# Hidden products of a mixture of experts: all three parts of each product in the same 160 PSUM columns, and the GELU reads PSUM

## The chip, the core and the metric

The kernel runs on one core of a Trainium2 chip. The metric is the device time of one launch in microseconds, the median of several runs. A core has TensorE (PE, with a weight load of its own that the profile lists as PEld), VectorE (DVE), ScalarE (ACT), GpSimd (POOL), SyncE (SP), and DMA queues.

## What is computed

The reference takes 1,250 nodes with 512 features, applies a layer norm, two graph convolutions and a three layer decoder, and adds the result to the input. The part that matters here comes after it: a dropless mixture of 8 experts over the first 512 tokens, two experts a token.

```
for e in range(NUM_EXPERTS):
    h = jax.nn.gelu(xg @ w1[e], approximate=False)
    y = jnp.where((bin_ids == e)[:, None], h @ w2[e], y)
w = expert_weights.reshape(-1)[order][:, None]
out = jnp.zeros((T, hs), x.dtype).at[token_ids].add(w * y)
```

Here `xg` are the normalised tokens sorted by expert, `w1` is 512 by 256 and `w2` 256 by 512 for each expert.

## The kernel before

The kernel is written by hand, engine by engine: each engine has a program of its own, in a fixed order, and the programs meet at semaphores. The graph part ends some 115 us into the span; the expert part, which the change touches, runs from there to the end.

**Tokens of an expert.** Each expert has 160 slots: 128 main slots, and 32 more (`MORE`) that hold what doesn't fit. Four experts (`TEAM`) share one tile of 128 for these extra slots, so there are two teams. The tokens of a slot list are gathered from memory by an indirect DMA (`gather`, L661), transposed by TensorE (`transpose_gathered`, L1859, and `transpose_tails`, L1869), and split in two parts: ScalarE copies the high part (`keep_gathered`, L1406 and L1411), and VectorE subtracts it from the transposed tokens to get the low part (`gathered_rest`, L1112 and L1116). The two parts of a tile lie side by side in `xg_t`, 160 columns each.

**Product up.** `up_slots(e)` makes the hidden units, 256 of them in two halves (m = 0, 1) of 128. Each half adds up, over four slices of the 512 features, high weight by high token, high weight by low token, and low weight by high token. Before, one product of 320 columns (L1886) takes the high weight against both token parts: the sum of high by high lands in columns 0 to 159 of bank 2 + m and that of high by low in columns 160 to 319. A product of 160 columns (L1889) then adds the low weight by high token to the first 160 columns. So a half is four products of 320 columns and four of 160 columns. After that ScalarE copies columns 160 to 319 to the tile `hs_part` (`keep_part`, L1426), VectorE adds columns 0 to 159 and writes `hs_raw` (`sum_hidden`, L1127), and ScalarE applies the GELU in place (L1444), rounds it to the high part `hs` (L1448) and applies the GELU of the 32 extra slots to `hs_tail` (L1450). VectorE subtracts for the low part of `hs` (L1150).

**Product down.** `down_slots(e)` (L1848, in `product`) is six products of 512 columns, scaled by VectorE (`keep_results`, L1135) and added to the output by an indirect DMA (`add_to_tokens`, L672). `down_tails(g)` (L1911) does the same for the extra slots of a team of four experts in 16 products; ScalarE scales the result (`keep_tails`, L1433), and `add_tails` on GpSimd adds it (L672 too).

**Orders that are fixed by hand.** TensorE, for each e: up(e+1), transposes of e+2 (and of a team's extra slots), down(e), and after the fourth and the last expert the extra slots' down. ScalarE, for each e: GELU of e, high part, GELU of the extra slots, high parts of the weights of expert e+3 (L1418), gathered tokens of e+2, `keep_part` of e+1, and for e = 4 the scaling `keep_tails(0)`; `keep_tails(1)` comes last. VectorE, for each e: low part of the up weights of e+2 (L1060), results of e-1 (L1135), low part of the hidden units (L1150), low part of the down weights (L1063), low part of the gathered tokens of e+2, `sum_hidden` of e+1. GpSimd: adds of experts 0 to 3 with three gathers between them, the add of the first team's extra slots, adds of experts 4 to 7, the add of the second team's extra slots. An add waits for the add two before it, and from expert 4 on also for the first team's add; the second team's add waits for that of expert 6. SyncE stores the rows of the graph part to the output, ten stores; GpSimd's first add waits for seven of them, and the seventh waits for the second expert's product up.

These are the waits between product up and its readers before: `up_slots(e)` waits for each half's sum of e-1 (`s_hs_sum`), since all experts share banks 2 and 3.

Of the kernel before, what the change touches and what calls it, by code (L numbers as in the profile page):

```python
# [29 lines left out]
ALU = mybir.AluOpType  # L30
# [8 lines left out]
P = 128  # L39
# [7 lines left out]
def gnn_moe(nc, x, src, dst, W1T, b1, W2T, b2, Wd1T, bd1, Wd2T, bd2, Wd3T, bd3, gate_w, gate_i,  # L47
# [62 lines left out]
    with ctx:  # L110
# [116 lines left out]
        xg = ring_flat[:, 0:XG * D].rearrange("p (b n) -> p b n", b=XG)  # L227
        tail = ring_flat[:, XG * D:(XG + TEAMS) * D].rearrange("p (g n) -> p g n", g=TEAMS)
        hs_at = (XG + TEAMS) * D
        hs_raw = ring_flat[:, hs_at:hs_at + KF * SLOTS].rearrange("p (k t) -> p k t", k=KF)  # L230
        hs_part = ring_flat[:, hs_at + KF * SLOTS:hs_at + 2 * KF * SLOTS].rearrange("p (k t) -> p k t", k=KF)
        hs_tail = ring_flat[:, hs_at + 2 * KF * SLOTS:hs_at + 2 * KF * SLOTS + TEAMS * KF * P].rearrange(
            "p (g k t) -> p g k t", g=TEAMS, k=KF)
        hs = at2_r[:, 4 * NP:4 * NP + 4 * KF * P].rearrange("p (b h k t) -> p b h k t", b=2, h=2, k=KF)
# [184 lines left out]
        s_xg_lo = sem("s_xg_lo")  # L419
        s_whi_act = sem("s_whi_act")  # L420
        s_up_sp = sem("s_up_sp")
        s_hs_part = sem("s_hs_part")
        s_hs_sum = sem("s_hs_sum")
        s_gelu_sp = sem("s_gelu_sp")
        s_hs_hi = sem("s_hs_hi")
        s_hs_lo = sem("s_hs_lo")
# [79 lines left out]
        def own_blocks(of, width):  # L506

            step = width + P
            flat = of[:, :, :].rearrange("p c n -> p (c n)")
            most = flat[:, 0:(CH - 1) * step].rearrange("p (c n) -> p c n", n=step)[:, :, 0:P]  # L510
            return most, flat[:, (CH - 1) * step:(CH - 1) * step + P].unsqueeze(1)

        def of_tails(e):

# [202 lines left out]
        def _(dve):  # L717
# [389 lines left out]
            with dve.If(sparse != 0):  # L1107
                def gathered_rest(e):

                    for i in range(2):  # L1110
                        dve.wait_ge(s_xg_hi, 3 * e + i + 1)
                        v.tensor_tensor(xg_t[:, e % 2, 2 * i:2 * i + 2, 1, 0:P],  # L1112
                                        bank[i][:, 0:2 * P].rearrange("p (k t) -> p k t", k=2),
                                        xg_t[:, e % 2, 2 * i:2 * i + 2, 0, 0:P].bitcast(F32), ALU.subtract).then_inc(s_xg_lo, 1)
                    dve.wait_ge(s_xg_hi, 3 * e + 3)
                    v.tensor_tensor(xg_t[:, e % 2, :, 1, P:], of_tails(e), xg_t[:, e % 2, :, 0, P:].bitcast(F32),  # L1116
                                    ALU.subtract).then_inc(s_xg_lo, 1)

                def sum_hidden(e):

                    if e >= 1:
                        dve.wait_ge(s_hs_hi, e)
                        dve.wait_ge(s_hs_lo, e)
                        dve.wait_ge(s_hs_tail, e)
                    for m in range(KF):
                        dve.wait_ge(s_hs_part, KF * e + m + 1)
                        v.tensor_tensor(hs_raw[:, m], bank[2 + m][:, 0:SLOTS], hs_part[:, m],  # L1127
                                        ALU.add).then_inc(s_hs_sum, 1)

                def keep_results(e):  # L1130

                    dve.wait_ge(s_down_sp, e + 1)
                    if e >= KEPT:
                        dve.wait_ge(s_added[(e - KEPT) % 2], 16 * ((e - KEPT) // 2 + 1))
                    v.tensor_scalar(y_out[e % KEPT], bank[4 + 2 * (e % 2)][:, 0:D], slot_weight[:, e:e + 1], None,  # L1135
                                    ALU.mult).then_inc(s_y, 1)

                dve.wait_ge(s_slot_weight, 1)
                gathered_rest(0)
                sum_rows(CH - 1)  # L1140
                gathered_rest(1)
                sum_hidden(0)
                for e in range(NE):
                    if e + 2 < NE:
                        dve.wait_ge(s_whi_act, 2 * (e + 1))
                        up_rest(e + 2)
                    if e >= 1:
                        keep_results(e - 1)
                    dve.wait_ge(s_hs_hi, e + 1)
                    v.tensor_tensor(hs[:, e % 2, 1], hs_raw[:, :, 0:P], hs[:, e % 2, 0].bitcast(F32), ALU.subtract).then_inc(s_hs_lo, 1)  # L1150
                    if 1 <= e < NE - 1:
                        down_rest(e + 1)
                    if e + 2 < NE:
                        gathered_rest(e + 2)
                    if e + 1 < NE:
                        sum_hidden(e + 1)
                keep_results(NE - 1)
            with dve.If(dense != 0):
                sum_rows(CH - 1)
# [27 lines left out]
        def _(act):  # L1187
# [211 lines left out]
            with act.If(sparse != 0):  # L1399
                def keep_gathered(e):  # L1400

                    if e >= 2:
                        act.wait_ge(s_up_sp, KF * (e - 1))
                    for i in range(2):
                        act.wait_ge(s_xgT, 2 * e + i + 1)
                        nc.scalar.copy(xg_t[:, e % 2, 2 * i:2 * i + 2, 0, 0:P],  # L1406
                                       bank[i][:, 0:2 * P].rearrange("p (k t) -> p k t", k=2)).then_inc(s_xg_hi, 1)
                    act.wait_ge(s_tailT, e // TEAM + 1)
                    if e >= 1:
                        act.wait_ge(s_xg_lo, 3 * e)  # L1410
                    nc.scalar.copy(xg_t[:, e % 2, :, 0, P:], of_tails(e)).then_inc(s_xg_hi, 1)  # L1411

                def first_parts(e):

                    if e >= W_HI + 1:
                        act.wait_ge(s_down_sp, e - W_HI)
                    for w, hi in zip(weights(e), weights_hi(e, W_HI + 1)):
                        nc.scalar.copy(hi, w).then_inc(s_whi_act, 1)  # L1418

                def keep_part(e):  # L1420

                    for m in range(KF):
                        act.wait_ge(s_up_sp, KF * e + m + 1)
                        if e >= 1:
                            act.wait_ge(s_hs_sum, KF * (e - 1) + m + 1)
                        nc.scalar.copy(hs_part[:, m], bank[2 + m][:, SLOTS:2 * SLOTS]).then_inc(s_hs_part, 1)  # L1426

                def keep_tails(g):

                    act.wait_ge(s_down_more, g + 1)  # L1430
                    if g >= 1:
                        act.wait_ge(s_added_more, 16 * g)
                    nc.scalar.activation(y_tail, bank[5][:, 0:D], ACT.Copy,  # L1433
                                         scale=slot_weight[:, NE + g:NE + g + 1]).then_inc(s_y_more, 1)

                act.wait_ge(s_ew, 16 * 2 * NE)
                act.wait_ge(s_slot_weight, 1)
                first_parts(2)
                keep_gathered(0)
                keep_gathered(1)  # L1440
                keep_part(0)
                for e in range(NE):
                    act.wait_ge(s_hs_sum, KF * (e + 1))
                    nc.scalar.activation(hs_raw[:, :, 0:P], hs_raw[:, :, 0:P], ACT.Gelu).then_inc(s_gelu_sp, 1)  # L1444
                    act.wait_ge(s_gelu_sp, e + 1)
                    if e >= 2:
                        act.wait_ge(s_down_sp, e - 1)
                    nc.scalar.copy(hs[:, e % 2, 0], hs_raw[:, :, 0:P]).then_inc(s_hs_hi, 1)  # L1448
                    q = e % TEAM * MORE
                    nc.scalar.activation(hs_tail[:, e // TEAM, :, q:q + MORE], hs_raw[:, :, P:], ACT.Gelu).then_inc(s_hs_tail, 1)  # L1450
                    if e + 3 < NE:
                        first_parts(e + 3)
                    if e + 2 < NE:
                        keep_gathered(e + 2)
                    if e + 1 < NE:
                        keep_part(e + 1)
                    if e % TEAM == 0 and e:
                        keep_tails(e // TEAM - 1)
                keep_tails(TEAMS - 1)
# [16 lines left out]
        def _(pe):  # L1476
# [374 lines left out]
            with pe.If(sparse != 0):  # L1851
# [20 lines left out]
                def up_slots(e):  # L1872
# [3 lines left out]
                    else:  # L1876
                        pe.wait_ge(s_wlo_up, e - 1)
                    pe.wait_ge(s_xg_lo, 3 * (e + 1))
                    for m in range(KF):
                        if e >= 1:  # L1880
                            pe.wait_ge(s_hs_sum, KF * (e - 1) + m + 1)


                        acc = bank[2 + m]
                        for k in range(KD):
                            mm(acc[:, 0:2 * SLOTS], w1_hi[:, k, m * P:(m + 1) * P],  # L1886
                               xg_t[:, e % 2, k].rearrange("p h t -> p (h t)"), start=(k == 0), stop=False)
                        for k in range(KD):
                            last = mm(acc[:, 0:SLOTS], w1_lo[:, e, k, m * P:(m + 1) * P], xg_t[:, e % 2, k, 0],  # L1889
                                      start=False, stop=(k == KD - 1))  # L1890
                        last.then_inc(s_up_sp, 1)

                def down_slots(e):
# [94 lines left out]
```

## Time and profile before

| | |
|---|---|
| median of 3 runs | 169.47 us (169.32 to 170.09) |
| the profiled execution's own time | 169.9 us |
| its span | 168.1 us, 3574 instructions |
| TensorE busy | 144.9 us (86% of the span) |
| VectorE busy | 130.9 us (78%) |
| ScalarE busy | 90.9 us (54%) |
| GpSimd busy | 41.4 us (25%) |
| TensorE's mean granted clock | 0.982 of full speed |

The span runs from the first to the last instruction, and the execution's own time holds 1.8 us more around it. Busy shares are averages over the whole span; the expert part has its own bounds, which only its own stretch of the trace tells. A matmul's recorded duration is longer than the time in which the next can start, so its cost in a row of products is read from start to start.

### The profile page before, as it was taken

How to read it: one execution, taken by the hardware profiler on the slowest of the kernel's cores; microseconds unless marked ns; L12 is line 12 of the kernel's file. 1: busy time of each engine (PE TensorE's matmuls, PEld its weight loads, DVE VectorE, ACT ScalarE, POOL GpSimd, SP SyncE). 2: the span in 40 equal slices, each digit the busy share in tenths (PEclk: the TensorE clock that was granted, in tenths of full speed). 3: DMA queues.
4: the chain of work that ended last, by engine and by line, in shares of the span. 5: the costliest groups of instructions: out<-in, count | busy, mean ns of one | idle time of the engine just before them, and what ended most of it. 6: DMA issues, size and time to landing. Idle time of an engine off the chain costs nothing.

```text
span 168.1 us, 3574 instructions
## 1 busy us (share of the span) xinstructions
PE 144.9 (86%) x1146; PEld 99.4 (59%) x1149; DVE 130.9 (78%) x317; ACT 90.9 (54%) x224; POOL 41.4 (25%) x57
## 2 busy tenths in 40 slices
PE   2968899999999999989999999899968999987500
PEld 1446677888788757546735444445957886875100
DVE  1899999999999789996469388399759999895100
ACT  3278777777788784013314506903588896653100
POOL 8300000000000000000000900078204877618550
PEclk9999999999999999999999999999999999999975
DMA  4999999994000000000000003335890986543874
GB/s 90 324 350 254 349 375 368 366 364 166 4 0 4 6 0 6 0 0 4 0 0 0 4 0 125 125 101 159 275 388 15 191 170 101 95 66 48 107 106 62
DMA packets 15355, 21.72 MB, mean 129 GB/s; under 512 B 2942, under 2 KB 7808, under 8 KB 15332
## 3 DMA queue, kind: packets, MB, share of 16 engines
q1 hardware_dynamic: 12994, 16.02, 28.7%
q0 software_dynamic: 2240, 5.24, 17.6%
q8 instruction: 13, 0.21, 0.5%
q10 hardware_dynamic: 98, 0.17, 0.3%
q14 instruction: 10, 0.08, 0.2%
HBM read 15.19 MB, written 6.23 MB: 127 GB/s over the span
## 4 chain that ended last, share of the span: by engine, by line
PE 45%; DVE 26%; ACT 9%; issue 7%; DMA 6%; POOL 2%; POOLq 1%; DVEq 0%; ACTq 0%
DVE ring L752 11%; PE bank L1560 9%; PE bank L1793 7%; DMA out<-at,to_i 6%; PE bank L1535 4%; PE bank L1886 3%; PE bank L1681 3%; PE bank L1889 2%; PE bank L1481 2%; PE bank L1819 2%; PE bank L1525 2%; DVE stats L1088 2%; PE bank L1848 2%; DVE x_sb L1082 2%; DVE ring L900 2%
## 5 line engine op out<-in xcount | busy, mean ns | idle before, releaser
L1560 PE MATMUL bank<-ring 128*128 128x110 bf16 x324 | 30.0, 222 | 3.9 <-DVE ring L752 2.7
L752 DVE TENSOR_TENSOR ring<-iota_slots,lo 128x1024 bf16<-128x1024 f16 (+1 forms) x41 | 27.4, 669 | 0.0
L1560 PEld LDWEIGHTS bank<-ring 128*128 128x128 bf16 x324 | 19.7, 98 | 11.9 <-issue 5.9
L658 POOL CAST at_r<-ew 128x1024 fp32r<-128x1024 f32 x4 | 4.6, 1183 | 83.6 <-PE bank L1810 83.6
L1266 ACT CAST at<-bank 128x400 f32 (+1 forms) x41 | 20.6, 503 | 7.5 <-PE bank L1566 6.7
L752 DVE TENSOR_TENSOR ring<-iota_dst,key 128x880 bf16<-128x880 f16 (+1 forms) x41 | 24.4, 594 | 0.0
L672 POOL DMA_INDIRECT out<-at,to_i x10 | 19.0, 1898 | 19.8 <-DVE at L1135 8.8
L1793 PE MATMUL bank<-wd3t_sb,at 128*128 128x512 f32 x40 | 17.9, 598 | 0.7 <-ACT at L1365 0.7
L1681 PE MATMUL bank<-at,ring 128*128 128x512 bf16 (+1 forms) x89 | 16.7, 343 | 0.1
L661 POOL DMA_INDIRECT ring<-x_rows,from_i x10 | 12.7, 1269 | 15.5 <-DMA x_rows<-at 12.8
L1886 PE MATMUL bank<-xnt_r,at_r 128*128 128x320 f32 x64 | 12.9, 323 | 2.9 <-DVE ring L1127 2.6
L1793 PEld LDWEIGHTS bank<-wd3t_sb,at 128*128 128x128 f32 x40 | 7.4, 190 | 10.0 <-issue 8.1
L1886 PEld LDWEIGHTS bank<-xnt_r,at_r 128*128 128x128 f32 x64 | 9.5, 189 | 6.0 <-issue 5.1
L1848 PE MATMUL bank<-at_r 128*128 128x512 f32 x32 | 11.9, 414 | 1.2 <-DVE at_r L1150 1.2
L1681 PEld LDWEIGHTS bank<-at,ring 128*128 128x128 bf16 x90 | 8.7, 98 | 7.0
L1418 ACT CAST at_r<-ew 128x1024 fp32r<-128x1024 f32 x12 | 11.9, 1037 | 0.0
L1535 PE MATMUL bank<-w1c,xnt 128*128 128x129 f32 x80 | 11.4, 284 | 0.0
L1082 DVE TENSOR_TENSOR x_sb<-x_sb,bank 128x512 f32<-128x512 f32 x10 | 6.8, 684 | 5.8 <-PE bank L1793 5.7
L1535 PEld LDWEIGHTS bank<-w1c,xnt 128*128 128x128 f32 x80 | 9.8, 191 | 0.1
L1889 PE MATMUL bank<-xnt_r,ew_r 128*128 128x160 f32 x64 | 9.2, 266 | 0.0
L1406 ACT CAST xnt_r<-bank 128x256 fp32r<-128x256 f32 x16 | 5.1, 372 | 7.3 <-PE bank L1859 7.3
L1889 PEld LDWEIGHTS bank<-xnt_r,ew_r 128*128 128x128 f32 x64 | 8.9, 190 | 0.0
(226 smaller groups left out, 267.0 us busy)
## 6 DMA issues: line engine op xcount, KB each, us to landing
ew<-in_w SPq DMA_DIRECT2D x16, 512.0 KB, 9.5
x_sb<-in_x SPq DMA_DIRECT2D x9, 256.0 KB, 5.0
out<-x_sb SPq DMA_DIRECT2D x9, 256.0 KB, 4.4
wd3t_sb<-in_Wd3T SPq DMA_DIRECT2D x1, 512.0 KB, 5.3
x_rows<-xn SPq DMA_DIRECT2D x1, 512.0 KB, 2.8
x_rows<-at SPq DMA_DIRECT2D x1, 512.0 KB, 2.8
w1t_sb<-in_W1T SPq DMA_DIRECT2D x1, 256.0 KB, 4.5
bd_sb<-in_bd SPq DMA_DIRECT2D x1, 256.0 KB, 4.5
```

Of the source, the lines that this page charges most:

```text
L661: nc.gpsimd.indirect_dma_start(to, None, x2_rows, bass.IndirectOffsetOnAxis(from_i[:, i:i + 1].bitcast(mybir.dt.uint32), 0)).then_inc(gath ...
L672: nc.gpsimd.indirect_dma_start(out[0:T + 3 * P, :], bass.IndirectOffsetOnAxis(to_i[:, i:i + 1].bitcast(mybir.dt.uint32), 0), of, None, com ...
L752: last = v.tensor_tensor(hot[:, slot, 0:tiles].rearrange("p t (n a) -> p t n a", a=2), lanes[:, 0:n].rearrange("p (n a) -> p n a", a=2).un ...
L1266: nc.scalar.copy(at[:, :, bass.ds(column, wide)], bank[j][:, 0:CH * wide].rearrange("p (c n) -> p c n", c=CH)).then_inc(s_placed, 1)
L1418: nc.scalar.copy(hi, w).then_inc(s_whi_act, 1)
L1535: last = mm(bank[6][:, 0:HID + 1], xnt[:, k, c * P:(c + 1) * P], w1c[:, k], start=(k == 0), stop=(k == KD - 1))
L1560: last = mm(to, hot_src[:, j, t], hot_dst[:, j, t], start=(t == 0 and not ends), stop=(first and t == tiles - 1), skip_group_check=not ends)
L1681: last = mm(bank[4 + i][:, 0:n], parts[k][:, s], at[:, s, a:a + n], start=(k == 0 and s == 0), stop=(k == last_k and s == CH - 1))
L1793: last = mm(bank[4 + c % 4][:, 0:D], y2t[:, k, c * P:(c + 1) * P], wd3t_sb[:, k], start=(k == 0), stop=(k == 1))
L1848: last = mm(acc, lhs(a, k), rhs(b, k), start=(i == 0), stop=(i == len(passes) - 1))
L1886: mm(acc[:, 0:2 * SLOTS], w1_hi[:, k, m * P:(m + 1) * P], xg_t[:, e % 2, k].rearrange("p h t -> p (h t)"), start=(k == 0), stop=False)
L1889: last = mm(acc[:, 0:SLOTS], w1_lo[:, e, k, m * P:(m + 1) * P], xg_t[:, e % 2, k, 0], start=False, stop=(k == KD - 1))
```

## The change

For each expert all three parts add up in the same 160 columns, and both halves lie side by side in one bank: bank 2 for even experts, bank 3 for odd ones. The 320 column product becomes two of 160 columns with the same weights, so that a half has 12 products of 160 columns and an expert 24, where it had 8 of 320 and 8 of 160. The GELUs read PSUM and write `hs_raw` (now 128 wide) and `hs_tail`; `keep_part` and `sum_hidden` go, with their two semaphores. `up_slots(e)` waits no longer for a sum; it waits for the extra slots' GELU of e-2, which is the last reader of its bank. The GELU of e waits for the low part of the hidden units of e-1, the last reader of `hs_raw`.

```diff
-        hs_raw = ring_flat[:, hs_at:hs_at + KF * SLOTS].rearrange("p (k t) -> p k t", k=KF)
-        hs_part = ring_flat[:, hs_at + KF * SLOTS:hs_at + 2 * KF * SLOTS].rearrange("p (k t) -> p k t", k=KF)
+        hs_raw = ring_flat[:, hs_at:hs_at + KF * P].rearrange("p (k t) -> p k t", k=KF)
...
+        def of_up(e):
+            return bank[2 + e % 2][:, 0:KF * SLOTS].rearrange("p (m t) -> p m t", m=KF)
...
-                def sum_hidden(e):
-
-                    if e >= 1:
-                        dve.wait_ge(s_hs_hi, e)
-                        dve.wait_ge(s_hs_lo, e)
-                        dve.wait_ge(s_hs_tail, e)
-                    for m in range(KF):
-                        dve.wait_ge(s_hs_part, KF * e + m + 1)
-                        v.tensor_tensor(hs_raw[:, m], bank[2 + m][:, 0:SLOTS], hs_part[:, m],
-                                        ALU.add).then_inc(s_hs_sum, 1)
...
-                    v.tensor_tensor(hs[:, e % 2, 1], hs_raw[:, :, 0:P], hs[:, e % 2, 0].bitcast(F32), ALU.subtract).then_inc(s_hs_lo, 1)
+                    v.tensor_tensor(hs[:, e % 2, 1], hs_raw, hs[:, e % 2, 0].bitcast(F32), ALU.subtract).then_inc(s_hs_lo, 1)
...
-                def keep_part(e):
-
-                    for m in range(KF):
-                        act.wait_ge(s_up_sp, KF * e + m + 1)
-                        if e >= 1:
-                            act.wait_ge(s_hs_sum, KF * (e - 1) + m + 1)
-                        nc.scalar.copy(hs_part[:, m], bank[2 + m][:, SLOTS:2 * SLOTS]).then_inc(s_hs_part, 1)
...
-                    act.wait_ge(s_hs_sum, KF * (e + 1))
-                    nc.scalar.activation(hs_raw[:, :, 0:P], hs_raw[:, :, 0:P], ACT.Gelu).then_inc(s_gelu_sp, 1)
+                    act.wait_ge(s_up_sp, KF * (e + 1))
+                    if e >= 1:
+                        act.wait_ge(s_hs_lo, e)
+                    nc.scalar.activation(hs_raw, of_up(e)[:, :, 0:P], ACT.Gelu).then_inc(s_gelu_sp, 1)
...
-                    nc.scalar.activation(hs_tail[:, e // TEAM, :, q:q + MORE], hs_raw[:, :, P:], ACT.Gelu).then_inc(s_hs_tail, 1)
+                    nc.scalar.activation(hs_tail[:, e // TEAM, :, q:q + MORE], of_up(e)[:, :, P:], ACT.Gelu).then_inc(s_hs_tail, 1)
...
+                    if e >= 2:
+                        pe.wait_ge(s_hs_tail, e - 1)
                     for m in range(KF):
-                        if e >= 1:
-                            pe.wait_ge(s_hs_sum, KF * (e - 1) + m + 1)
...
-                        acc = bank[2 + m]
+                        acc = of_up(e)[:, m]
+                        rows = [xg_t[:, e % 2, k] for k in range(KD)]
                         for k in range(KD):
-                            mm(acc[:, 0:2 * SLOTS], w1_hi[:, k, m * P:(m + 1) * P],
-                               xg_t[:, e % 2, k].rearrange("p h t -> p (h t)"), start=(k == 0), stop=False)
+                            for h in range(2):
+                                mm(acc, w1_hi[:, k, m * P:(m + 1) * P], rows[k][:, h], start=(k == 0 and h == 0), stop=False)
                         for k in range(KD):
-                            last = mm(acc[:, 0:SLOTS], w1_lo[:, e, k, m * P:(m + 1) * P], xg_t[:, e % 2, k, 0],
-                                      start=False, stop=(k == KD - 1))
+                            last = mm(acc, w1_lo[:, e, k, m * P:(m + 1) * P], rows[k][:, 0], start=False, stop=(k == KD - 1))
                         last.then_inc(s_up_sp, 1)
```

## Rows read from the trace of the kernel before

**Rows 1.** Chain that ended last: start us, us, what (waits merged)

```profile
144.30 0.59 ACT at L1433
...
145.67 4.77 DMA out<-at,to_i
...
151.18 5.23 DMA out<-at,to_i
```

**Rows 2.** GpSimd's timeline: start us, us, engine line op, idle before

```profile
128.03 2.08 POOL L672 DMA_INDIRECT out<-at,to_i  x1 [8.83 <-DVE at L1135]
...
141.91 2.13 POOL L672 DMA_INDIRECT out<-at,to_i  x1 [0.60 <-issue]
...
162.22 1.55 POOL L672 DMA_INDIRECT out<-at,to_i  x1 [1.65 <-DMA out<-at,to_i]
```

**Rows 3.** ScalarE's timeline around the first team's scaling, same columns

```profile
143.08 0.65 ACT L1406 CAST xnt_r<-bank 128x256 fp32r<-128x256 f32 x2 [0.84 <-PE bank L1859]
...
143.77 0.53 ACT L1426 COPY ring<-bank 128x160 f32<-128x160 f32 x2
144.14 0.74 ACT L1433 ACTIVATE at<-bank,slot_weight 128x512 f32<-128x512 f32 x1
```

**Rows 4.** TensorE's timeline, experts 1 to 5, same columns

```profile
119.85 0.78 PE L1886 MATMUL bank<-xnt_r,at_r 128*128 128x320 f32 x4
...
121.91 0.61 PE L1859 MATMUL bank<-ident,ring 128*128 128x128 f32 x4
122.31 0.47 PE L1848 MATMUL bank<-at_r 128*128 128x512 f32 x1
...
125.27 0.82 PE L1886 MATMUL bank<-xnt_r,at_r 128*128 128x320 f32 x4 [1.32 <-DVE ring L1127]
...
127.73 0.48 PE L1848 MATMUL bank<-at_r 128*128 128x512 f32 x1
...
129.92 0.82 PE L1886 MATMUL bank<-xnt_r,at_r 128*128 128x320 f32 x4 [0.54 <-DVE ring L1127]
130.58 0.57 PE L1889 MATMUL bank<-xnt_r,ew_r 128*128 128x160 f32 x4
130.99 0.78 PE L1886 MATMUL bank<-xnt_r,at_r 128*128 128x320 f32 x4
...
132.82 0.48 PE L1848 MATMUL bank<-at_r 128*128 128x512 f32 x1
...
134.57 0.83 PE L1886 MATMUL bank<-xnt_r,at_r 128*128 128x320 f32 x4
...
137.04 0.47 PE L1848 MATMUL bank<-at_r 128*128 128x512 f32 x1
...
138.61 1.92 PE L1911 MATMUL bank<-ew,ring 128*32 128x512 f32 x16
...
142.60 0.61 PE L1859 MATMUL bank<-ident,ring 128*128 128x128 f32 x4
```

**Rows 5.** Timeline: weight loads of one run of eight narrow products (129 columns)

```profile
47.76 0.97 PEld L1535 LDWEIGHTS bank<-w1c,xnt 128*128 128x128 f32 x8
```

**Rows 6.** Lines by themselves: durations ns min/median/max; L1681 reuses its weights in threes

```profile
L1535 PEld LDWEIGHTS bank<-w1c,xnt x80: 186/192/198, 15.7 to 55.3; 128*128 128x128 f32 x80
...
L1681 PEld LDWEIGHTS bank<-at,ring x90: 95/98/153, 59.2 to 80.1; 128*128 128x128 bf16 x90
L1681 PE MATMUL bank<-at,ring x89: 271/379/379, 59.2 to 80.2; 128*128 128x512 bf16 x59, 128*128 128x256 bf16 x30
```

**Rows 7.** VectorE's timeline: a sum, the tokens of expert 6, a result

```profile
134.11 0.55 DVE L1127 TENSOR_TENSOR ring<-bank,ring 128x160 f32<-128x160 f32 x2
...
143.49 0.76 DVE L1112 TENSOR_TENSOR xnt_r<-bank,xnt_r 128x256 fp32r<-128x256 f32 x2 [0.92 <-ACT xnt_r L1406]
144.16 0.28 DVE L1116 TENSOR_TENSOR xnt_r<-bank,xnt_r 128x128 fp32r<-128x128 f32 x1
...
153.14 0.75 DVE L1135 TENSOR_SCALAR at<-bank,slot_weight 128x512 f32<-128x512 f32 x1 [0.70 <-PE bank L1848]
```

More of the change, by code:

```diff
@@ L421, in gnn_moe @@
         s_up_sp = sem("s_up_sp")
-        s_hs_part = sem("s_hs_part")
-        s_hs_sum = sem("s_hs_sum")
         s_gelu_sp = sem("s_gelu_sp")
@@ L1141, in _ @@
                 gathered_rest(1)
-                sum_hidden(0)
                 for e in range(NE):
@@ L1154, in _ @@
                         gathered_rest(e + 2)
-                    if e + 1 < NE:
-                        sum_hidden(e + 1)
                 keep_results(NE - 1)
@@ L1440, in _ @@
                 keep_gathered(1)
-                keep_part(0)
                 for e in range(NE):
-                    act.wait_ge(s_hs_sum, KF * (e + 1))
-                    nc.scalar.activation(hs_raw[:, :, 0:P], hs_raw[:, :, 0:P], ACT.Gelu).then_inc(s_gelu_sp, 1)
+                    act.wait_ge(s_up_sp, KF * (e + 1))
+                    if e >= 1:
+                        act.wait_ge(s_hs_lo, e)
+                    nc.scalar.activation(hs_raw, of_up(e)[:, :, 0:P], ACT.Gelu).then_inc(s_gelu_sp, 1)
                     act.wait_ge(s_gelu_sp, e + 1)
@@ L1447, in _ @@
                         act.wait_ge(s_down_sp, e - 1)
-                    nc.scalar.copy(hs[:, e % 2, 0], hs_raw[:, :, 0:P]).then_inc(s_hs_hi, 1)
+                    nc.scalar.copy(hs[:, e % 2, 0], hs_raw).then_inc(s_hs_hi, 1)
                     q = e % TEAM * MORE
-                    nc.scalar.activation(hs_tail[:, e // TEAM, :, q:q + MORE], hs_raw[:, :, P:], ACT.Gelu).then_inc(s_hs_tail, 1)
+                    nc.scalar.activation(hs_tail[:, e // TEAM, :, q:q + MORE], of_up(e)[:, :, P:], ACT.Gelu).then_inc(s_hs_tail, 1)
                     if e + 3 < NE:
@@ L1454, in _ @@
                         keep_gathered(e + 2)
-                    if e + 1 < NE:
-                        keep_part(e + 1)
                     if e % TEAM == 0 and e:
```

## Prediction

> **What bounds the kernel now.** I read the chain that ended last first, because the engines' busy shares average over stages. Its end is a string of indirect adds to the output, each waiting for one before it [rows 1, 2]. The first team's add is issued at 145.67 and takes 4.77 us to land; expert 4's add goes at 151.18 and takes 5.23 us; expert 6's add follows its landing, and the second team's add starts at 162.22. The span ends at 168.1, so 22.4 us pass between the issue at 145.67 and the end, and hardly any of it is arithmetic. The question for every edit is therefore when the add at 145.67 can be issued.
>
> GpSimd itself is ready then: its previous add started at 141.91 and took 2.13 us, to 144.04 [rows 2]. What is late is ScalarE's scaling of the first team's rows, 144.14 to 144.88, and 0.79 us of issue follow it. Its operand is no cause either: TensorE's 16 products for it started at 138.61 and took 1.92 us [rows 4]. The scaling is queued on ScalarE behind the copies of the gathered tokens of expert 6, which wait for TensorE, and behind the two copies that the change removes, 143.77 to 144.14 [rows 3]. The tokens' copies start 0.48 us after the transposes at 142.60 [rows 3, 4]. In TensorE's order these transposes stand behind six products up (experts 0 to 5), four products down and the team's own. So the path is: TensorE's work to 142.60, 0.48, copies 0.69, the copies to be removed 0.37, scaling and issue 1.53, adds 22.4.
>
> Is TensorE full on that stretch? Not quite [rows 4]. A product down that nothing holds up takes 1.57 us from start to start (137.04 to 138.61). From expert 0's down to expert 2's up it is 122.31 to 125.27, 1.39 us more; then 127.73 to 129.92, 0.62 more; then 132.82 to 134.57, 0.18 more. That is 2.19 us of waiting for VectorE's sums. Down to expert 5's product I find no other wait.
>
> **The change, part by part.** *TensorE, product up.* Before, 119.85 to 121.91: 2.06 us for 8 products of 320 columns and 8 of 160 [rows 4]. After: 24 products of 160. The cheap reading is the group of four at 130.58, whose successor starts at 130.99: 0.41 us, 0.103 each [rows 4]. But each such group follows four wide products, behind which its first loads are hidden. In a long run of narrow ones the weight loads set the pace. The trace has such a run [rows 5, 6]: eight loads of 128 columns of fp32 weights take 0.97 us, and with 0.19 us for a single one they come every (0.97 - 0.19) / 7 = 0.111 us, with 129 columns streamed, fewer than 160. I take 0.111 to 0.112, since 24 alike are nearer to this run than to groups of four. 24 x 0.112 = 2.69 us, 0.63 more an expert. The bounds: 0.103 each gives 2.47, 0.41 more; no extra cost gives 2.06.
>
> The number of loads doesn't shrink because two products in a row share their weights: on another line, whose three products in a row do, 90 loads stand against 89 products [rows 6].
>
> A product of 160 columns should cost less by a rule of the Trainium skill (TensorE: Matmul & The Clock Gate, Back-to-back issue gap): the gap is the columns over 2.4 GHz plus 2.5 ns, 69 ns here. Both versions stream 3,840 columns an expert, so by that rule the cost is the same. The same page's LDWEIGHTS section has 107 ns for a load of 128 columns, which would make 24 of them 2.57 us; rows 5 agree with that one, within 5 ns a load.
>
> *TensorE, waits.* Up(e) no longer waits for a sum, but for the gathered tokens' low parts. From the start of the transposes these take 0.48 to ScalarE's copy, 0.41 more to VectorE (143.08 to 143.49), 0.67 and 0.28 there [rows 3, 4, 7]: 1.84 us. TensorE in the meantime has transposes (0.40, 121.91 to 122.31) and a product down (1.57), 1.97 us. So it arrives later than the data, by 0.1 us, and its waits go, all 2.19. The new wait for the extra slots' GELU of e-2 is met a whole round earlier, and costs nothing; the covering round is 4.66 us.
>
> *VectorE.* The two sums take 0.55 us [rows 7] of a round of 4.65 us (129.92 to 134.57 [rows 4]). A round without them is about 4.1 us, below TensorE's new 2.69 + 0.40 + 1.57 = 4.66. Here the bound changes: VectorE's saving buys nothing, because TensorE takes its place. Removing the sums is costed at nothing beyond the waits above.
>
> *ScalarE.* The GELU of e starts when both halves are done, without a copy and a sum of the second half ahead of it. It reads PSUM; 256 columns from PSUM (0.65 us for two copies [rows 3]) are no dearer than what it did from SBUF, so zero, bounded by 0.1 us either way. It is early for expert 4, because the tokens' copies behind it wait for TensorE anyway. Its wait for the low part of e-1 is met long before. On the path ScalarE loses only the copies at 143.77: 0.37 us.
>
> *The other queues.* GpSimd's first add also needs seven stores, and the seventh waits for the up of expert 1, which now ends 2 x 0.63 = 1.3 us later. That can move GpSimd's chain, 128.03 to 144.04, by about 1.3 us, to 145.3 [rows 2]. It hides behind the scaling, which now comes later than that.
>
> *Sum.* Six products up at 0.63: +3.78. Waits filled: -2.19. Copies ahead of the scaling: -0.37. Together **+1.22 us**: the add is issued at 146.9. Behind it nothing is tight: expert 6's result, scaled at 153.14 [rows 7], is needed when expert 4's add lands, then at 157.6. In the new order the downs of 4, 5 and 6 and the ups of 6 and 7 bring it to 144.2 (142.60 + 1.59) + 0.8 + 4.7 + 5.4 + 0.7 = 155.8 at the earliest, 1.8 us early. The span becomes 169.3 us. The profiled execution, 169.9 us, stands 0.43 above the median of the runs; I put the change on the median: 169.47 + 1.2 = 170.7.
>
> **The rivals.** (1) *The group price holds:* 0.103 us a product. Then +2.46 - 2.19 - 0.37 = -0.1: no change, 169.3 us. For it: 64 narrow products in this very part have it. Against it: the run of rows 5. Chance 0.16.
>
> (2) *TensorE costs the same as before* and the change is faster. Either time goes by columns, or the second product with the same weights is not loaded again, so that the change's 24 products hold 16 loads. Then TensorE's round is 4.03 us and VectorE's 4.1, and most of the 2.19 goes to the end: the scaling would be ready some 2 us sooner. GpSimd then decides. If its chain stays, the add is issued at 144.3, 1.3 us sooner; if its first add also comes 1 us sooner, 2.3. That gives 167.2 to 168.2, and I take 167.6. It decides as soon as a product costs less than about 0.10 us. Against it: rows 5 and 6. The Trainium skill's rule of columns, above, is this rival. Chance 0.12.
>
> (3) *The pace of loads holds, and the adds land later as well.* Landings in this part are 4.8 to 5.2 us [rows 1]; four of them are on the path, and 0.3 more each gives 171.9 us. Nothing in the change asks for it, except that the seventh store is later, nearer to the first add. Chance 0.07.
>
> **How the numbers follow.** The forecast has 0.62; the remaining 0.03 is for an earlier scaling than I see. A measurement of this kernel can tell about 0.5% from no change, that is 0.85 us: slower starts at 170.32. The forecast's own range is 169.9 (0.107 us a product: 3.06 - 2.19 - 0.37 = +0.5) to 171.2, and four fifths of it lie past 170.32. Slower: 0.62 x 0.8 + 0.07 = 0.57. Same: 0.62 x 0.2 + 0.16 x 0.85 = 0.26. Faster: 0.12 and the rest, 0.17. The range takes in the price of groups at its low end and late landings at its high end, 169.0 to 171.9, and leaves out rival 2.
>
> **What would show it.** Right: 24 products of 160 columns at 2.6 to 2.75 us an expert; no idle time of TensorE ahead of product up; transposes of expert 6 at 144.2, scaling of the first team at 145.3, its add at 146.9, 22.4 us to the end as before. GELUs of experts 1 to 3 start earlier than before, without use. Wrong: 2.1 to 2.5 us an expert, or transposes of expert 6 before 143, or an add that waits for something other than the scaling, such as GpSimd's own queue.

## The result and the profile after

The change makes the kernel a little slower: 170.38 us against 169.70, the median of six runs each, a ratio of 1.0046 with a 95% interval of 1.003 to 1.0063. By the ratio that is 0.8 us (0.5 to 1.1), by the medians 0.7, where 1.2 us were forecast. It is a loss clear of the interval, and in size it lies just inside the 0.5% that the prediction called no change; the forecast's figure was 170.7 us, on the 169.47 us of the first three runs. The profiled execution took 170.72 us with a span of 169.0, 0.9 us more than the span before.

TensorE's timeline after the change, the stretch of [rows 4] (start us, us, engine line op):

```profile
120.44 1.06 PE L1863 MATMUL bank<-xnt_r,at_r 128*128 128x160 f32 x8
...
123.13 0.61 PE L1836 MATMUL bank<-ident,ring 128*128 128x128 f32 x4
123.49 0.48 PE L1825 MATMUL bank<-at_r 128*128 128x512 f32 x1
...
125.07 1.09 PE L1863 MATMUL bank<-xnt_r,at_r 128*128 128x160 f32 x8
...
128.15 0.48 PE L1825 MATMUL bank<-at_r 128*128 128x512 f32 x1
...
129.72 1.09 PE L1863 MATMUL bank<-xnt_r,at_r 128*128 128x160 f32 x8
...
133.25 0.48 PE L1825 MATMUL bank<-at_r 128*128 128x512 f32 x1
...
134.72 1.02 PE L1863 MATMUL bank<-xnt_r,at_r 128*128 128x160 f32 x8
...
139.30 1.92 PE L1886 MATMUL bank<-ew,ring 128*32 128x512 f32 x16
...
143.91 0.61 PE L1836 MATMUL bank<-ident,ring 128*128 128x128 f32 x4
```

The product up of expert 1 now takes 120.44 to 123.13, 2.69 us, where it took 2.06 [rows 4]: 24 products every 0.112 us. After the first, no product up shows idle time ahead of it any more; from the start of a product down to the start of the next product up it is 1.58, 1.57 and 1.47 us, where it was 2.96, 2.19 and 1.75. The transposes of expert 6 start at 143.91, 1.31 us later than before.

ScalarE's timeline after, the place of [rows 3], then GpSimd's, as [rows 2] and the adds of [rows 1]:

```profile
144.39 0.65 ACT L1392 CAST xnt_r<-bank 128x256 fp32r<-128x256 f32 x2 [2.98 <-PE bank L1836]
144.92 0.28 ACT L1397 CAST xnt_r<-bank 128x128 fp32r<-128x128 f32 x1
145.08 0.71 ACT L1411 ACTIVATE at<-bank,slot_weight 128x512 f32<-128x512 f32 x1
```

```profile
127.64 2.08 POOL L672 DMA_INDIRECT out<-at,to_i  x1 [8.46 <-DVE at L1124]
...
141.80 2.13 POOL L672 DMA_INDIRECT out<-at,to_i  x1 [0.60 <-issue]
146.59 1.74 POOL L672 DMA_INDIRECT out<-at,to_i  x1 [2.66 <-ACT at L1411]
152.07 2.19 POOL L672 DMA_INDIRECT out<-at,to_i  x1 [3.74 <-DVE at L1124]
...
157.89 1.55 POOL L672 DMA_INDIRECT out<-at,to_i  x1 [1.77 <-DMA out<-at,to_i]
...
163.04 1.55 POOL L672 DMA_INDIRECT out<-at,to_i  x1 [1.46 <-DMA out<-at,to_i]
```

The scaling follows the tokens' copies at once. GpSimd is ready for the first team's add at 143.93 and waits 2.66 us for ScalarE. From that add to the end of the span it is 22.4 us, as before. One reading needs care: the row at 152.07 names VectorE as what the add of expert 4 waited for. That result was scaled from 146.79 to 147.54, long before. What came last was the landing of the add at 146.59, for the add of expert 4 waits for both: it landed 4.7 us after its issue, at 151.3, and the next issue followed 0.8 us later; before it was 4.8 and 0.7.

VectorE's timeline after shows who is now the bound, and how early expert 6's result is:

```profile
133.33 0.76 DVE L1112 TENSOR_TENSOR xnt_r<-bank,xnt_r 128x256 fp32r<-128x256 f32 x2 [0.44 <-ACT xnt_r L1392]
...
154.86 0.75 DVE L1124 TENSOR_SCALAR at<-bank,slot_weight 128x512 f32<-128x512 f32 x1 [2.03 <-PE bank L1825]
```

VectorE waits 0.44 us a round for the copies of transposes that TensorE makes late. Expert 6's result is ready at 155.61, and its add goes at 157.89.

### The profile page after: what moved, and what is told of

Its sections match the earlier page's. It is cut to its first block, busy times and chain, and to the rows that moved or that the text cites. A ratio compares the mean times of both kernels' runs of the same rounds, so it can differ in the third digit from the quotient of the medians.

```text
span 169.0 us, 3649 instructions
## 1 busy us (share of the span) xinstructions
PE 148.7 (88%) x1210; PEld 104.1 (62%) x1213; DVE 127.2 (75%) x301; ACT 87.0 (52%) x208; POOL 41.8 (25%) x57
## 4 chain that ended last, share of the span: by engine, by line
PE 53%; DVE 28%; issue 5%; ACT 4%; DMA 3%; POOL 3%; POOLq 1%; DVEq 0%; ACTq 0%
DVE ring L752 13%; PE bank L1863 8%; PE bank L1537 8%; PE bank L1770 7%; PE bank L1825 5%; PE bank L1865 4%; PE bank L1512 4%; DMA out<-at,to_i 3%; PE bank L1658 3%; PE bank L1458 2%; PE bank L1836 2%; PE bank L1796 2%; DVE stats L1088 2%; DVE x_sb L1082 2%; DVE ring L900 2%
## 5 line engine op out<-in xcount | busy, mean ns | idle before, releaser
L1863 PE MATMUL bank<-xnt_r,at_r 128*128 128x160 f32 x128 | 17.1, 277 | 0.2 <-DVE xnt_r L1116 0.2
L1863 PEld LDWEIGHTS bank<-xnt_r,at_r 128*128 128x128 f32 x128 | 15.6, 192 | 2.7 <-issue 1.8
L1112 DVE TENSOR_TENSOR xnt_r<-bank,xnt_r 128x256 fp32r<-128x256 f32 x16 | 6.0, 418 | 6.5 <-ACT xnt_r L1392 6.5
L1865 PE MATMUL bank<-xnt_r,ew_r 128*128 128x160 f32 x64 | 9.8, 275 | 0.0
```

Of the source, the lines that this page charges most:

```text
L1863: mm(acc, w1_hi[:, k, m * P:(m + 1) * P], rows[k][:, h], start=(k == 0 and h == 0), stop=False)
L1865: last = mm(acc, w1_lo[:, e, k, m * P:(m + 1) * P], rows[k][:, 0], start=False, stop=(k == KD - 1))
```

## The experiments

Each run is compared with the kernel before on the same chip.

**1. Only the products made narrow.** The kernel before with its 320 column product in two pieces; copy and sum stay.

```diff
-                            mm(acc[:, 0:2 * SLOTS], w1_hi[:, k, m * P:(m + 1) * P],
-                               xg_t[:, e % 2, k].rearrange("p h t -> p (h t)"), start=(k == 0), stop=False)
+                            for h in range(2):
+                                mm(acc[:, h * SLOTS:(h + 1) * SLOTS], w1_hi[:, k, m * P:(m + 1) * P],
+                                   xg_t[:, e % 2, k, h], start=(k == 0 and h == 0), stop=False)
```

> The kernel before with its 320 column product issued as two of 160 columns with the same weights, into the two column ranges as before; copy, sum and their waits stay. Theory (weight loads pace the narrow products, the end hangs on the first team's scaling): product up takes 2.69 us an expert instead of 2.06, TensorE still waits for sums, and the copy still stands ahead of the scaling. Six ups at 0.62 are +3.7, of which the waits can absorb some 1.2, because the sums are later too: scaling at 146.6, time +2.3 to +2.6 us (171.9 to 172.3 on a base of 169.7). Rival (time goes by columns streamed, or a repeated weight isn't loaded again): product up stays at 2.1 us and the time within 0.3 us of before. Second rival (the narrow products cost what the trace shows, but the change's loss comes from later stores or adds): product up 2.69, yet scaling and time within 1 us of before.

Measured: 172.87 us against 169.62, ratio 1.0186 (1.0169 to 1.0203), 3.2 us more. Rows of its timelines, TensorE, then ScalarE and GpSimd:

```profile
120.95 1.06 PE L1887 MATMUL bank<-xnt_r,at_r 128*128 128x160 f32 x8
...
122.29 1.06 PE L1887 MATMUL bank<-xnt_r,at_r 128*128 128x160 f32 x8
...
123.63 0.61 PE L1859 MATMUL bank<-ident,ring 128*128 128x128 f32 x4
...
126.37 1.09 PE L1887 MATMUL bank<-xnt_r,at_r 128*128 128x160 f32 x8 [0.72 <-DVE ring L1127]
...
131.31 1.09 PE L1887 MATMUL bank<-xnt_r,at_r 128*128 128x160 f32 x8 [0.22 <-DVE ring L1127]
```

```profile
147.32 0.74 ACT L1433 ACTIVATE at<-bank,slot_weight 128x512 f32<-128x512 f32 x1
```

```profile
148.86 1.80 POOL L672 DMA_INDIRECT out<-at,to_i  x1 [2.58 <-ACT at L1433]
```

Expert 1's product up takes 120.95 to 123.63, 2.68 us. That is the change's price with nothing else of the change in it, so the price belongs to the products, not to the shared columns or to the GELU. Both rivals fall. The size was missed, 3.2 us for 2.3 to 2.6. In the profiled execution the part began 0.5 us late (its first product up at 118.24; in its first 20 us the granted clock was 0.91, and 1.00 in the kernel before), and from there the first team's add is 2.7 us later than before. The waits for the sums absorbed 0.9 of the six ups' 3.6 us, where 1.2 were expected; 0.72 and 0.22 us of them are still there. Whether the other executions began late as well, and lose the rest of the 3.2 us there, no trace shows.

**2. One part left out.** The changed kernel with 16 products an expert.

```diff
-                            for h in range(2):
+                            for h in range(1):
```

> The changed kernel without the products of high weights by low tokens: that part of the hidden units is left out, 16 narrow products an expert instead of 24, everything else as changed. Theory: product up 16 x 0.112 = 1.79 us, so TensorE's round is 3.8 us and VectorE's 4.2 us sets the pace; the scaling is ready at about 141.8, and GpSimd's own chain (16.3 us from its first add to the end of its fourth) decides: first add some 1 us sooner, the team's add at 143 to 144.3, time 1.3 to 2.4 us below before (167.3 to 168.4). Rival (the removed sum and copy are worth nothing here, because the end is bound by the landings from an earlier point): time within 0.4 us of before. Second rival (the GELU from PSUM or the new waits cost something): the ups are still spaced 4.6 us apart.

Measured: 165.81 us against 169.62, ratio 0.979 (0.9772 to 0.9808), 3.8 us less. TensorE's, ScalarE's and GpSimd's timelines:

```profile
123.97 0.65 PE L1863 MATMUL bank<-xnt_r,at_r 128*128 128x160 f32 x4 [0.58 <-issue]
...
128.09 0.65 PE L1863 MATMUL bank<-xnt_r,at_r 128*128 128x160 f32 x4 [0.29 <-issue]
...
132.22 0.65 PE L1863 MATMUL bank<-xnt_r,at_r 128*128 128x160 f32 x4
```

```profile
141.06 0.72 ACT L1411 ACTIVATE at<-bank,slot_weight 128x512 f32<-128x512 f32 x1
```

```profile
129.08 1.00 POOL L661 DMA_INDIRECT ring<-x_rows,from_i  x1 [0.30 <-issue]
...
138.84 2.13 POOL L672 DMA_INDIRECT out<-at,to_i  x1 [0.60 <-issue]
142.58 1.73 POOL L672 DMA_INDIRECT out<-at,to_i  x1 [1.61 <-ACT at L1411]
```

The rounds are 4.12 us apart, VectorE's pace without the sums, as the prediction had it (4.1), and TensorE has idle time again. So what the change takes off VectorE and ScalarE is worth several us as soon as TensorE doesn't take its place; both rivals fall. The 3.8 us are an upper bound of it, because TensorE's product up, 1.79 us here, is also shorter than the 2.06 of the kernel before. The gain is larger than the 1.3 to 2.4 us that were expected. GpSimd was not the bound that I made it: its chain took 13.8 us here (127.15 to 140.97), not 16. Its gathers took 1.0 to 1.1 us, not 1.6, so the scaling still decides, at 141.06, and the add goes at 142.58, not at 143 or later. Another 1.0 us came from the end: 21.4 us from the add to the end of the span, where it was 22.4. It lies in two landings: from expert 4's add to expert 6's, and from there to the last one, it took 5.0 us each, where it was 5.5. Why they landed sooner isn't shown.

**3. The same 24 products with fewer columns.** In the changed kernel all three `mm` calls use the first 96 columns.

```diff
-                                mm(acc, w1_hi[:, k, m * P:(m + 1) * P], rows[k][:, h], start=(k == 0 and h == 0), stop=False)
+                                mm(acc[:, 0:96], w1_hi[:, k, m * P:(m + 1) * P], rows[k][:, h, 0:96], start=(k == 0 and h == 0), stop=False)
...
-                            last = mm(acc, w1_lo[:, e, k, m * P:(m + 1) * P], rows[k][:, 0], start=False, stop=(k == KD - 1))
+                            last = mm(acc[:, 0:96], w1_lo[:, e, k, m * P:(m + 1) * P], rows[k][:, 0, 0:96], start=False, stop=(k == KD - 1))
```

> The changed kernel with its 24 products streaming 96 columns instead of 160: the hidden units of slots 96 to 159 are left out, all else is as changed. Theory (weight loads set the pace): a product up still takes 24 x 0.112 = 2.69 us, the span stays within 0.3 us of the changed kernel's. Rival (time goes by columns): 24 x (96/2.4 + some 30 ns) = 1.7 to 1.9 us, and the span falls by over 1.5 us.

Measured in one execution: span 168.8 us, where the changed kernel has 169.0. TensorE's timeline:

```profile
120.44 1.06 PE L1863 MATMUL bank<-xnt_r,at_r 128*128 128x96 f32 x8
...
123.12 0.64 PE L1836 MATMUL bank<-ident,ring 128*128 128x128 f32 x4
```

and its weight loads':

```profile
120.40 0.97 PEld L1863 LDWEIGHTS bank<-xnt_r,at_r 128*128 128x128 f32 x8
```

120.44 to 123.12 is 2.68 us with 96 columns, 2.69 with 160. The columns streamed cost nothing here. What is left is a price for each product with its weight load, and the loads come at that pace: eight in 0.97 us, one every 0.111, as in [rows 5]. No run changed the load alone, so that it is the load, and not another fixed cost of each product, is the likely reading and not a shown one; the change pays the same either way. The two sections of the Trainium skill that the prediction set against each other (TensorE: Matmul & The Clock Gate) don't contradict each other: Back-to-back issue gap gives its formula by columns for a product by itself, and says that in a stream of loads and products both set the spacing. Its sustained 81 ns a product at 128 columns is not what these fp32 weights gave, 112 ns at 96 and at 160 columns; here the measurement decides. The 107 ns of its section LDWEIGHTS for 128 columns stand beside 112 ns measured.

**4. The scaling ahead of the tokens' copies**, on the kernel before and on the changed one.

```diff
+                    if e % TEAM == 0 and e:
+                        keep_tails(e // TEAM - 1)
                     if e + 2 < NE:
                         keep_gathered(e + 2)
...
-                    if e % TEAM == 0 and e:
-                        keep_tails(e // TEAM - 1)
```

> The kernel before with the first team's scaling on ScalarE moved ahead of the copies of expert 6's gathered tokens. Theory: the scaling starts when TensorE's team products are done and ScalarE is through its weights, at about 142.2 instead of 144.1, and is ready at 142.9; the team's add is then bound by GpSimd, whose add before it ends at 144.04: issue at 144.3 instead of 145.67, time 1.3 us less (168.4 on a base of 169.7). Rival (another wait sets the end, for example the landings of experts 2 to 5): time unchanged within 0.3 us.

> The changed kernel with the same move. Theory: the scaling starts at 141.6 instead of 145.1, the team's add at about 144.2 instead of 146.6, bound by GpSimd. But then a new wait shows: expert 6's result is scaled only at 154.9 to 155.6, and its add must wait for that (about 156.4) rather than for the landing at 155.2. So 1.2 to 1.5 us below the changed kernel, 0.5 to 1.2 us above the kernel before with the move. Rival (the loss of the change lies wholly in the place of the scaling): both kernels with the move have the same time within 0.2 us.

Measured: on the kernel before 168.58 us against 169.67, ratio 0.9932 (0.9907 to 0.9957), 1.1 us less; on the changed kernel 169.93 us, ratio 1.0008 (0.9985 to 1.0031), 0.45 us below the change's 170.38 (0.6 by the two ratios), where 1.2 to 1.5 were expected. GpSimd's timeline of the first:

```profile
141.91 2.13 POOL L672 DMA_INDIRECT out<-at,to_i  x1 [0.60 <-issue]
144.35 1.58 POOL L672 DMA_INDIRECT out<-at,to_i  x1 [0.30 <-issue]
...
155.43 1.55 POOL L672 DMA_INDIRECT out<-at,to_i  x1 [1.80 <-DMA out<-at,to_i]
```

and GpSimd's and VectorE's of the second:

```profile
144.08 1.58 POOL L672 DMA_INDIRECT out<-at,to_i  x1 [0.30 <-issue]
...
156.23 1.55 POOL L672 DMA_INDIRECT out<-at,to_i  x1 [2.13 <-DVE at L1124]
...
162.25 1.55 POOL L672 DMA_INDIRECT out<-at,to_i  x1 [1.63 <-DMA out<-at,to_i]
```

```profile
154.69 0.75 DVE L1124 TENSOR_SCALAR at<-bank,slot_weight 128x512 f32<-128x512 f32 x1 [2.01 <-PE bank L1825]
```

This shows where the end hangs in the kernel before: moving one ScalarE instruction brings the first team's add from 145.67 to 144.35, 1.3 us, and the time down by 1.1. It also shows that the change's loss is not only its effect on the scaling. In the changed kernel the add moves by 2.5 us, to 144.08, but expert 6's result, ready at 155.44, then holds its add: it goes at 156.23, 1.7 us sooner than 157.89. That is the new wait that was expected, within 0.2 us. Half of these 1.7 us is gone at the last add, the second team's: it is issued 6.0 us after expert 6's, where it was 5.15, and so 0.8 us sooner than in the changed kernel. The span is 0.8 us shorter, the median of the runs 0.45. With the scaling out of the way the change costs 1.35 us (169.93 against 168.58), a little over the 0.5 to 1.2 that were expected; the rival, no difference, falls.

**5. A gather issued early as well.** GpSimd issues expert 5's gather ahead of its first add.

```diff
                 gather(4)
+                gather(5)
...
-                    if e + XG + 2 < NE:
+                    if 1 <= e and e + XG + 2 < NE:
```

> The kernel before with the scaling moved and GpSimd's gather of expert 5 issued ahead of the first add, in the time in which GpSimd waits for it. Theory: GpSimd's chain is shorter by one gather, 1.9 us: its fourth add ends at 142.1, the team's add is issued at 143 (scaling ready 142.9, 0.8 us of issue), 2.0 us less than with the move alone would be bound by landings, but expert 6's result at 153.9 holds its add at about 154.7 instead of 156.68: time 2.0 us below before (167.7). Rival: the gather collides with the stores that the first add waits for, and the first add starts later by as much: no gain over the move alone.

> The changed kernel with both moves. Theory: the add of expert 6 waits for its result (155.6) and goes at 156.4, so nothing is gained over the changed kernel with the scaling moved, and it stands 1.5 to 2 us above the kernel before with both moves: TensorE's 0.62 us an expert is then paid in full for experts 0 to 7 less the waits. Rival (cost hidden again): within 0.5 us of the kernel before with both moves.

Measured: 169.02 us (0.9944, 0.9913 to 0.9974) on the kernel before, where 167.7 was expected, and 170.06 (1.0022, 1.0004 to 1.004) on the changed one: nothing gained over experiment 4. My theory of GpSimd's chain falls, and not by the rival's mechanism. GpSimd's timeline, kernel before with both moves:

```profile
128.03 2.08 POOL L672 DMA_INDIRECT out<-at,to_i  x1 [4.30 <-DVE at L1136]
132.08 2.65 POOL L672 DMA_INDIRECT out<-at,to_i  x1 [1.97 <-DVE at L1136]
...
141.86 2.15 POOL L672 DMA_INDIRECT out<-at,to_i  x1 [0.54 <-issue]
```

The first add starts when it did. The second comes only 0.2 us sooner though the gather between them is gone, because it waits 1.97 us for VectorE's result. The adds are paced by the results, one round apart, and GpSimd's chain only looked full. The trace of the kernel before could have told: its results of experts 2 and 3 end at 136.46 and 141.11, and their adds start 0.80 us later each, at 137.26 and 141.91 [rows 2], though the view puts that idle time down to "issue".

```profile
135.71 0.75 DVE L1135 TENSOR_SCALAR at<-bank,slot_weight 128x512 f32<-128x512 f32 x1
...
140.36 0.75 DVE L1135 TENSOR_SCALAR at<-bank,slot_weight 128x512 f32<-128x512 f32 x1
```

```profile
137.26 2.12 POOL L672 DMA_INDIRECT out<-at,to_i  x1 [0.60 <-issue]
```

On the changed kernel it went as expected: nothing gained over experiment 4, and expert 6's add at 156.41, held by its result. But it stands 1.0 us above the kernel before with both moves, not 1.5 to 2, since that one gained nothing.

**6. The results scaled earlier on VectorE**, with the scaling of experiment 4.

```diff
+                    if e >= 1:
+                        keep_results(e - 1)
                     if e + 2 < NE:
                         dve.wait_ge(s_whi_act, 2 * (e + 1))
                         up_rest(e + 2)
-                    if e >= 1:
-                        keep_results(e - 1)
```

> The kernel before with the first team's scaling moved ahead, and on VectorE the results of e-1 scaled ahead of the up weights' low part of e+2 (1.13 us sooner). Theory (with the scaling out of the way GpSimd's adds are paced by VectorE's results): the first add starts at about 127.0 (stores landed at 126.2) instead of 128.0, the fourth add ends at 143.0, the team's add goes at 143.3 to 143.6 instead of 144.35, so 0.8 to 1.0 us below the kernel with the scaling moved alone (167.6 to 167.8 on a base of 169.7). Rival (GpSimd's chain is paced by something else, such as the stores): team's add at 144.3, no gain over the scaling alone.

> The changed kernel with the same two moves. Theory: the add of expert 6 waits for TensorE (its down product ends at about 154.7), which no move on VectorE or GpSimd brings forward: add at 156.2, time within 0.3 us of the changed kernel with the scaling moved (169.6 to 170.2 on a base of 169.7). Rival (the changed kernel is bound by the same adds as the one before): it falls by 0.8 us too, to 169.1.

Measured: 168.75 us against 169.68 (0.9933, 0.9912 to 0.9955) and 170.00 (1.0021, 1.0006 to 1.0035). On the kernel before 167.6 to 167.8 were expected. GpSimd's timeline of the first:

```profile
127.27 1.73 POOL L672 DMA_INDIRECT out<-at,to_i  x1 [8.05 <-DMA out<-x_sb]
129.31 0.99 POOL L661 DMA_INDIRECT ring<-x_rows,from_i  x1 [0.30 <-issue]
...
143.65 1.58 POOL L672 DMA_INDIRECT out<-at,to_i  x1 [1.06 <-ACT at L1433]
...
154.72 1.55 POOL L672 DMA_INDIRECT out<-at,to_i  x1 [1.28 <-DMA out<-at,to_i]
...
160.90 1.55 POOL L672 DMA_INDIRECT out<-at,to_i  x1 [1.79 <-DMA out<-at,to_i]
```

The results come earlier, and the second to fourth adds with them, 1.1 to 1.4 us sooner than in experiment 4: that the results pace them is shown. The first team's add comes at 143.65, as the theory had it, and expert 6's at 154.72, 0.7 us sooner than in experiment 4. The time doesn't follow: the last add is at 160.90, against 160.75 there, 6.2 us after expert 6's, against 5.3. The mechanism held, the gain did not. On the changed kernel the expectation held (169.6 to 170.2).

So the kernel before with its scaling moved has the lowest median, 168.58 us, 1.1 below the kernel before and 1.8 below the changed one. The two further moves on it, 169.02 and 168.75, can't be told apart from it: the intervals of their ratios overlap.

## Why the prediction was right

**The price of a narrow product** was the step on which everything hung, and it held: 0.112 us against the forecast's 0.111 to 0.112. It came from a run of eight loads elsewhere in the trace [rows 5, 6], not from the nearer groups of four [rows 4], whose 0.103 would have given no change (rival 1). Experiment 3 shows that columns don't set it, experiment 1 that it is the narrow products alone. Rival 2, no extra cost, falls with them; experiment 2 gives an upper bound of what it would have been worth. The GELU cost nothing from PSUM, as forecast: 0.42 us for 256 columns, as it took in place before.

**The term that was too large** is the six ups: +3.78 forecast. Measured from start to start, they cost 0.60, 0.63, 0.61, 0.63, 0.53 and 0.61 us more, 3.61 in all. I had taken the old price from expert 1's product up, 2.06 us, the only one that follows another; the other five took 2.10 to 2.14.

**The waits filled** were put at 2.19 us, and the three downs became 1.38, 0.62 and 0.28 us shorter, 2.28. With 0.02 from small steps TensorE's path is 1.31 us longer, not 1.59. **The copies ahead of the scaling** gave 0.37: transposes to scaling was 1.54 us and is 1.17. Scaling to add is 1.51 us, 0.02 less than before. So the add is issued 0.92 us later, at 146.59; 146.9 was forecast. **Behind it** nothing was tight: 22.4 us to the end in both, so rival 3, later landings, falls too. The span shows +0.9, the timed medians +0.7 (and the ratio 0.8); the forecast of +1.2 was too high by the 0.3 us of the first two terms, which erred the same way, and the medians differ by less than the spans because the profiled execution stands 0.34 us above its median, where that of before stood 0.2.

**The chances beside the sum** were less well founded. The range's upper end, 171.2, has no working, and by length about two thirds of 169.9 to 171.2 lie past 170.32, not four fifths. Whether the result counts as slower or as no change hangs on the base: 170.38 is past the 170.32 that was worked out from 169.47, but within 0.5% of 169.70.

**Who becomes the bound** held: VectorE's savings bought nothing but the waits. The GELUs of experts 1 to 3 began up to 1.1 us earlier, without use.

**What was wrong beside the sum** is the picture of GpSimd. I took its row of back to back transfers for a chain with a length of its own, 16 us. Experiments 2, 5 and 6 show that it isn't: in 2 and 6 the gathers shrink to 1.0 to 1.1 us, and in 5 and 6 the adds follow VectorE's results. The fear that the seventh store, now later, would hold the first add was empty too: that add came 0.4 us sooner. Neither was on the path of this change, so the forecast survived; that was luck, for this part. In experiment 2 the same picture had the add at 143 or later, and it went at 142.58.

## What to carry to other kernels

Cutting a wide product in two to spare an addition elsewhere doubles its weight loads, here from 8 to 16 an expert. Before doing it, price the narrow product from the longest run of equally narrow ones in the trace, not from a short group behind wide ones, and see whether the engine that is relieved is the one that the end waits for. And look at what is queued in front of the instruction on the path: here one instruction moved on ScalarE was worth more, 1.1 us, than the change cost.

## What the runs showed of the hardware

In runs of 24 narrow products, each with 128 columns of fp32 weights, one came every 0.110 to 0.115 us with 160 columns streamed and every 0.109 to 0.113 with 96. The granted clock was 1.00 in this stretch, that is 2.4 GHz.

GpSimd's transfer instructions had no fixed length: beside the first adds a gather took 0.99 to 1.1 us in some kernels and 1.6 to 1.9 us in others (in experiment 1 both, 1.88, 0.99 and 1.91), and an add 1.55 to 2.65 us. VectorE's work was placed differently beside them; which of it matters wasn't tried.

From the issue of expert 6's add to that of the last one it took 5.0 to 5.5 us in seven of the eleven profiles of this study (5.54 before, 5.15 after) and 5.7 to 6.2 in four: experiments 4, 5 and 6 on the changed kernel, and experiment 6 on the kernel before. In those four expert 7's add was issued 2.8 us after expert 6's, in the other seven 1.9 to 2.6. Whether that is the cause stays open; it is of the size of the gains that didn't arrive.
